# Attention scores from 49 contracted rows, two heads at a time on the two halves of the partitions

## The reference

```python
# layer 0
h = layer_norm(x) * (1 + scale) + shift          # scale, shift from the condition
scores = q @ k.T / sqrt(16) - torus_dist * torus_scale[head]
x = x + softmax(where(mask, scores, -1e30)) @ v @ Wout
x = x + gelu(layer_norm(x) @ W1 + b1) @ W2 + b2
# layer 1
scores = where(node_mask, q @ k.T / sqrt(16), -inf)
x = x + gate * modulate(layernorm(softmax(scores) @ v @ proj_w + proj_b))
x = x + gate * modulate(layernorm(gelu(x @ fc1_w + fc1_b) @ fc2_w + fc2_b))
```

## Time and profile before

| | |
|---|---|
| median of 3 runs | 1530.71 us (1530.26 to 1530.89) |
| profiled execution | 1530.74 us, of it 1528.9 between first and last instruction |
| mean granted TensorE clock | 0.96 of full |
| PE / PEld busy | 1372.1 / 1090.1 us |
| DVE / ACT / POOL busy | 866.8 / 803.0 / 692.0 us |
| first score product of turn 0 | at 43.42 us |
| scores of layer 0 | until 869.7 us, of layer 1 from 887.6 us |

### The profile page before, as it was taken

How to read it: one execution, slowest core, us unless ns; L and a number is a source line. 1 busy time by engine, 2 the same in 40 slices (tenths; PEclk the granted TensorE clock), 3 DMA queues, 4 the chain that set the end, 5 groups by cost and what they waited for, 6 DMA issues and landing times.

```text
span 1528.9 us, 25914 instructions
## 1 busy us (share of the span) xinstructions
PE 1372.1 (90%) x9365; PEld 1090.1 (71%) x9365; DVE 866.8 (57%) x2296; ACT 803.0 (53%) x1266; POOL 692.0 (45%) x856
## 2 busy tenths in 40 slices
PE   5898999999999999999999978898979888888867
PEld 3666777777777777777777767676767677767655
DVE  3766647548548457466556454647384746465551
ACT  3556655756746746656657526362535444453611
POOL 2788767758658758668768510101010101010110
PEclk9999999999999999999999989998999998999988
DMA  8654426325425534345263275856665747474510
GB/s 252 109 112 76 92 29 98 84 30 98 98 41 79 103 55 72 84 76 98 37 117 85 29 161 84 180 89 137 93 154 73 160 62 166 56 158 79 69 42 14
DMA packets 102537, 142.56 MB, mean 93 GB/s; under 512 B 22114, under 2 KB 49906, under 8 KB 102402
## 3 DMA queue, kind: packets, MB, share of 16 engines
q1 hardware_dynamic: 102402, 140.82, 49.6%
HBM read 98.27 MB, written 41.98 MB: 92 GB/s over the span
## 4 chain that ended last, share of the span: by engine, by line
PE 56%; DVE 18%; ACT 12%; POOL 7%; issue 3%; DMA 2%; SPq 1%; DVEq 0%; ACTq 0%; POOLq 0%
PE dense L589 15%; PE dense L569 13%; PE turned L669 9%; DVE shifted L1082 5%; PE pv L684 5%; PE score L657 4%; POOL shifted L472 3%; PE score L703 3%; ACT hidden L853 2%; PE turned L712 2%; POOL bias L465 2%; ACT L853 2%; DVE stats L968 2%; ACT L888 2%; DVE x_norm L978 2%
## 5 line engine op out<-in xcount | busy, mean ns | idle before, releaser
L1082 DVE CUSTOM_DVE_ANT_0 shifted<-score,bias 128x512 f32<-128x512 f32 x512 | 332.7, 687 | 258.4 <-PE score L657 156.8
L472 POOL TENSOR_SCALAR shifted<-shifted,row_max 128x512 f32<-128x512 f32 x512 | 358.3, 712 | 222.1 <-DVE row_max L1082 219.9
L872 ACT ACTIVATE probs<-turned 128x512 f32<-128x512 f32 x512 | 278.1, 596 | 213.3 <-PE turned L669 211.7
L669 PE MATMUL turned<-ident,shifted 128*128 128x128 f32 x2048 | 269.7, 274 | 7.5 <-POOL shifted L472 6.8
L669 PEld LDWEIGHTS turned<-ident,shifted 128*128 128x128 f32 x2048 | 233.3, 141 | 56.5 <-issue 26.7
L589 PE MATMUL dense<-w_down,hidden 128*128 128x256 f32 x1024 | 247.0, 385 | 12.1 <-ACT hidden L853 12.1
L465 POOL TENSOR_SCALAR bias<-dist,scale 128x1024 f32<-128x1024 f32 x192 | 218.4, 1138 | 21.0 <-DMA down_bias<-in_L_cond_b 21.0
L657 PE MATMUL score<-k_rows,q_rows 65*128 65x512 f32 x512 | 205.3, 456 | 23.6 <-DVE row_max L1082 10.5
L589 PEld LDWEIGHTS dense<-w_down,hidden 128*128 128x128 f32 x1024 | 185.6, 191 | 51.1 <-issue 16.3
L569 PE MATMUL dense<-feat_m,w_up 128*128 128x512 f32 x768 | 192.7, 404 | 8.4 <-DVE feat_m L1046 6.1
L888 ACT ACTIVATE probs<-turned 128x512 f32<-128x512 f32 x128 | 76.4, 597 | 202.8 <-PE turned L712 202.4
(11 more groups left out here) (114 smaller groups left out, 1556.6 us busy)
## 6 DMA issues: line engine op xcount, KB each, us to landing
q_rows<-qk_halves SPq DMA_DIRECT2D x256, 128.0 KB
k_rows<-qk_halves SPq DMA_DIRECT2D x256, 128.0 KB
qk_halves<-qk_high SPq DMA_DIRECT2D x64, 256.0 KB, 3.0
qk_halves<-qk_low SPq DMA_DIRECT2D x64, 256.0 KB, 3.0
x_in_t<-in_x SPq DMA_DIRECT2D x8, 512.0 KB, 3.6
x_res<-in_x SPq DMA_DIRECT2D x8, 512.0 KB, 8.3
x_mid<-x_norm SPq DMA_DIRECT2D x8, 512.0 KB, 3.5
x_in_t<-x_mid SPq DMA_DIRECT2D x8, 512.0 KB, 9.1
```

The costliest lines, as they stand in the source:

```text
L472: ins = pool.tensor_scalar(shifted[:, u % 3, i, :], shifted[:, u % 3, i, :], -1.0, row_max[:, t % 6:t % 6 + 1], ALU.mult, ALU.add)
L669: mm = pe.transpose(turned_bank[z % 2][:, HALF * kk + P * i:HALF * kk + P * i + P], shifted[:, u % 3, i, P * kt:P * kt + P], ident[:, :])
L872: act.activation(probs[:, u % RING, 2 * pair:2 * pair + 2, :], turned_bank[z % 2][:, :].rearrange("p (a c) -> p a c", a=2), ACT.Exp)\
L1082: dve.tensor_tensor_reduce(shifted[:, u % 3, i, :], score_bank[t % 2], bias[:, u % 2, i, :], 1.0, 3.0e38, ALU.add, ALU.min, row_max[:, t % ...
```

## The change

- The low x low term goes: 3 x 16 rows and the mask's row, 49 in place of 65.
- Even heads lie on partitions 0 to 48 and odd heads on 64 to 112 of `q_rows` and `k_rows`. A group is loaded by 14 transfers instead of 9 (12 of 16 rows by two heads, two of the mask's row). The ones are set on two ranges of 32 partitions.
- A unit of layer 0 is now one tile of 128 queries of two heads (`unit(u)`), in the two banks as before. Both its products wait until both tiles of the unit before have been read.
- Its bias is made by two instructions of 128 x 512, since the scale differs by head.
- `pv` takes its 256 queries from two units (two runs of 128 columns).
- In layer 1 the scores of two heads are made at even steps, one head to a bank, 4 pairs of products of 256, 256, 256 and 128 columns.

```diff
-    KROWS = 4 * HD
+    TERMS = ((0, 0), (0, 1), (1, 0))
+    KROWS = len(TERMS) * HD
+    STRIP = P // 2
-    ROWS_LOADED = 9 * 16
+    ROWS_LOADED = 2 * (2 * len(TERMS) + 1) * 16
+    def unit(u):
+        return HG * (u // 8) + 2 * (u % 4 // 2), 2 * (u // 4 % 2) + u % 2
...
-        q_rows = sb("q_rows", [KROWS + 1, 2, HG, L], F32R)
-        k_rows = sb("k_rows", [KROWS + 1, 2, HG, L], F32R)
+        q_rows = sb("q_rows", [P, 2, HG // 2, L], F32R)
+        k_rows = sb("k_rows", [P, 2, HG // 2, L], F32R)
...
             def load_group(m, g):
-                for r in range(4):
-                    sp.dma_start(q_rows[HD * r:HD * r + HD, g % 2, :, :].bitcast(F32),
-                                 qk_halves[m, r // 2, 0, rows, :].rearrange("(h e) n -> e h n", e=HD))\
+                for e in range(2):
+                    for r, (x, y) in enumerate(TERMS):
+                        at = slice(STRIP * e + HD * r, STRIP * e + HD * r + HD)
+                        sp.dma_start(q_rows[at, g % 2, :, :].bitcast(F32),
+                                     qk_halves[m, x, 0, rows, :].rearrange("(h a e) n -> a e h n", a=2, e=HD)[e])\
+                            .then_inc(loaded, 16)
...
             def make_bias(n, u):
-                pool.tensor_scalar(bias[:, u % 2, :, :], dist[:, 2 * half:2 * half + 2, :], scale[:, h:h + 1], 0.0,
-                                   ALU.mult, ALU.add).then_inc(s["bias_ready"], 1)
+                for i in range(2):
+                    ins = pool.tensor_scalar(bias[:, u % 2, i, :], dist[:, tile, :], scale[:, h + i:h + i + 1], 0.0,
+                                             ALU.mult, ALU.add)
+                ins.then_inc(s["bias_ready"], 1)
...
             def scores(n, u):
+                if n > 0 or u > 0:
+                    pe.wait_ge(s["scores_used"], TILES * n + 2 * u)
                 for i in range(2):
-                    t = 2 * u + i
-                    if n > 0 or t > 1:
-                        pe.wait_ge(s["scores_used"], TILES * n + t - 1)
-                    q0 = HALF * half + P * i
-                    pe.matmul(score_bank[t % 2], q_rows[:, g % 2, j, q0:q0 + P],
-                              k_rows[:, g % 2, j, :], start=True, stop=True).then_inc(s["scores_ready"], 1)
+                    at = slice(STRIP * i, STRIP * i + KROWS + 1)
+                    pe.matmul(score_bank[i], q_rows[at, g % 2, pair, P * tile:P * tile + P],
+                              k_rows[at, g % 2, pair, :], start=True, stop=True).then_inc(s["scores_ready"], 1)
...
             def attend(n, gq):
+                        slot = (4 * gq + j // 2 * 2) % RING
-                                       probs[:, (4 * gq + j) % RING, kt, :], start=(kt == 0), stop=(kt == TT - 1),
+                                       probs[:, slot:slot + 2, kt, P * (j % 2):P * (j % 2) + P], start=(kt == 0), stop=(kt == TT - 1),
...
             def head_scores_of(n, h):
                 pe.wait_ge(s["scores_used"], TILES * n + TT * h)
-                for t in range(TT):
-                    mm = pe.matmul(score[:, t // 2, HALF * (t % 2):HALF * (t % 2) + HALF],
-                                   q_rows[:, g % 2, j, P * t:P * t + P], k_rows[:, g % 2, j, L - HALF:L],
-                                   start=True, stop=True)
-                mm.then_inc(s["scores_ready"], TT)
+                for t in reversed(range(TT)):
+                    first = max(t - 1, 0)
+                    for i in range(2):
+                        at = slice(STRIP * i, STRIP * i + KROWS + 1)
+                        mm = pe.matmul(score_bank[i][:, P * first:P * t + P],
+                                       q_rows[at, g % 2, pair, P * t:P * t + P],
+                                       k_rows[at, g % 2, pair, L - P * (t + 1 - first):L], start=True, stop=True)
+                mm.then_inc(s["scores_ready"], 2 * TT)
...
-                        if k < H:
+                        if k < H and k % 2 == 0:
                             head_scores_of(n, k)
```

More of the change, by code:

```diff
@@ L127, in build @@
         score_bank = [score[:, i, :] for i in range(2)]
-        head_scores = score[:, :, :].rearrange("p a b -> p (a b)").rearrange("p (t k) -> p t k", t=TT)[:, :, HALF - P:HALF]
+        head_scores = [score[:, i, :].rearrange("p (t k) -> p t k", t=TT) for i in range(2)]
         turned_bank = [ps(f"turned{i}") for i in range(2)]
@@ L294, in load_mask @@
                 rows = d["mask_BxS_bf1"] if m < B else d["mask_BxS_bk0"]
-                sp.dma_start(mask_row[KROWS:KROWS + 1, :], rows[m % B:m % B + 1, :]).then_inc(s["mask_loaded"], 16)
+                sp.dma_start(mask_row[:, :], rows[m % B:m % B + 1, :]).then_inc(s["mask_loaded"], 16)
                 if m >= B:
@@ L317, in load_group @@
                 rows = slice(HG * HD * g, HG * HD * (g + 1))
-                for r in range(4):
-                    sp.dma_start(q_rows[HD * r:HD * r + HD, g % 2, :, :].bitcast(F32),
-                                 qk_halves[m, r // 2, 0, rows, :].rearrange("(h e) n -> e h n", e=HD))\
-                        .then_inc(loaded, 16)
[L322 to L327, removed]
+                for e in range(2):
[4 more added lines that the diff above has]
+                            .then_inc(loaded, 16)
+                        sp.dma_start(k_rows[at, g % 2, :, :].bitcast(F32),
+                                     qk_halves[m, y, 1, rows, :].rearrange("(h a e) n -> a e h n", a=2, e=HD)[e])\
+                            .then_inc(loaded, 16)
+                    at = STRIP * e + KROWS
+                    sp.dma_start(k_rows[at:at + 1, g % 2, :, :].bitcast(F32),
+                                 mask_neg[:, :].bitcast(F32).unsqueeze(1).broadcast_to([1, HG // 2, L]))\
+                        .then_inc(loaded, 16)
             def next_mask(m):
@@ L512, in prologue @@
                 pool.wait_ge(s["pool_consts"], 3)
-                pool.memset(q_rows[KROWS:KROWS + 1, :, :, :].bitcast(F32), 1.0).then_inc(s["ones_set"], 1)
-                pool.wait_ge(s["ones_set"], 1)
+                for e in range(2):
+                    pool.memset(q_rows[STRIP * e + 32:STRIP * e + STRIP, :, :, :].bitcast(F32), 1.0)\
+                        .then_inc(s["ones_set"], 1)
+                pool.wait_ge(s["ones_set"], 2)
                 mask(0)
@@ L648, in scores @@
             def scores(n, u):
[L649 removed]
+                h, tile = unit(u)
+                g, pair = h // HG, h % HG // 2
                 if u % 8 == 0:
                     rows_loaded(n, g)
+                if n > 0 or u > 0:
+                    pe.wait_ge(s["scores_used"], TILES * n + 2 * u)
                 for i in range(2):
[L653 to L658 removed]
+                    at = slice(STRIP * i, STRIP * i + KROWS + 1)
+                    pe.matmul(score_bank[i], q_rows[at, g % 2, pair, P * tile:P * tile + P],
+                              k_rows[at, g % 2, pair, :], start=True, stop=True).then_inc(s["scores_ready"], 1)
             def turn_unit(n, u):
@@ L856, in make_bias @@
             def make_bias(n, u):
-                h = HG * (u // 8) + u % 4
-                half = u // 4 % 2
+                h, tile = unit(u)
                 if n > 0 or u > 1:
                     act.wait_ge(s["scores_used"], TILES * n + 2 * u - 2)
-                act.activation(bias[:, u % 2, :, :], dist[:, 2 * half:2 * half + 2, :], ACT.Copy,
-                               scale=scale[:, h:h + 1]).then_inc(s["act_bias_ready"], 1)
+                for i in range(2):
+                    ins = act.activation(bias[:, u % 2, i, :], dist[:, tile, :], ACT.Copy, scale=scale[:, h + i:h + i + 1])
+                ins.then_inc(s["act_bias_ready"], 1)
             def exps(n, u):
```

21 lines of the change are left out of this document (10 added, 11 removed).

## The result

The changed kernel takes 1543.8 us, median of 4 runs (1541.6 to 1547.0); the kernel before took 1530.5 on the same chip (4 runs, 1529.9 to 1530.9). The ratio is 1.0089, with an interval of 1.0067 to 1.0111: slower by 13 us. The profiled execution took 1547.0 us with a span of 1545.1, so it is the longest of the four, and its differences from before are some 3 us larger than those of the medians.

The account below looks back on a forecast made before the run. It took the first layer as bound by TensorE's instruction stream, the second by a chain that changes engines. Against 1530.74 us, +28 (first layer) - 16 (second) + 1 (loading) = +13: 1544 us; whole range 1506 to 1566.

Parts of the forecast that it names:

- Step 1: Layer 0's split score pair on TensorE: edges make it 0.12 us longer per pair, 0.035 less where `pv` follows.
- The 0.38 among the signs: Sign in the profile after: transposes come 0.38 us from where the score pair starts to stream.
- Free edges: Rival: the row split needs no emptying of the array, weights are still loaded ahead; 1502 us, chance 0.17.
- half price: Rival: the array is drained at the split's edges, but weights are preloaded; 1525 us, chance 0.18.
- Strips in turn: Rival: strips load one after the other, each pair has 0.10 more exposed; 1561 us, chance 0.13.
- no sharing: Rival: a pair's two products share nothing, 0.235 us more for some 19 pairs; 1584 us, chance 0.06.
- Step 2: Layer 0's wait for both tiles: 0.62 us added VectorE idle per place; 1.0, 0.8 and 0.8 late at three stretches.
- less rounding: Deduction for places that overlap, in layer 0's sum 1.0 + 0.8 + 0.8 + 0.9 + 0.15, giving +3.5 us a turn.
- Step 3: Two-instruction bias in layer 0: GpSimd's +0.29 us each mostly ready in time; two ScalarE biases on the chain, +0.15 a turn.
- GpSimd becomes what VectorE waits for: Sign that would show the forecast wrong: VectorE waiting for GpSimd, whose bias was put near 0.7 us twice.
- Step 4: Layer 1's scores of both heads at even steps, none at odd: -2.0 us a turn, 8 turns, -16 us.
- Step 5: Loading before the first score product: +2.3 us if issue decides, -2.6 if bytes do; taken as +1.

Follow-up runs that it names:

- the first experiment: The changed kernel, but in layer 0 each score product waits for its own bank alone: 1528.2 us, ratio 1.0012 to the kernel before.
- bias alone: The kernel before, with each bias made by two instructions of 128x512 on GpSimd and ScalarE and nothing else: 1539.6 us, ratio 1.0076.
- 49 rows alone: The kernel before, low x low term left out, 49 rows contracted from partition 0 for every head, products one after another: 1589.8 us, ratio 1.0406.
- no split: The changed kernel, but layer 0's score products contract rows 0 to 112, so the array is not split there: 1539.3 us, ratio 1.0068 to the kernel before.
- both-tile wait alone: The kernel before, with both score products of a unit waiting until both tiles of the unit before are read: 1556.3 us, ratio 1.018.
- three terms over 65 rows: The kernel before, low x low term left out, still 65 rows with rows 48 to 63 zeros, 7 transfers for 9: 1523.9 us, ratio 0.9971.

## Why the prediction was right, and where its terms were not

**The time.** 1544.0 predicted, 1543.8 measured; a layer-0 turn of 111.1 predicted, 111.3 measured. The forecast's mechanism holds in kind: edges on both sides of each pair cost more than the sharing gives, the wait for both tiles costs more than they do, and layer 1 gives back some 40%. The total is nearer than its terms deserve. In the profiled execution layer 0 lost 31.6 us for 28, layer 1 gained 12.8 for 16, and the start gained 2.55 where 1 was to be lost.

**Step 1, the pair on TensorE: right, 0.12 predicted, 0.13 measured.** By parts: entry 0.10, not 0.20; from the pair's start to the transposes 0.43, where the sum had 0.235 and 0.10; behind it 0.05, as put. (The 0.38 among the signs takes in that 0.05, which doesn't lie there.) Where `pv` follows it is 0.42 after an entry of 0.10, for 0.47 and 0.10: 0.05 less, put at 0.035. For a turn I had 1.06, 0.86 after the waits for ScalarE; the first experiment less the bias alone gives 109.9 - 108.68 = 1.2. That is a difference, not a run: no run has the split pairs alone, and edges and bias overlap in part (the table below, unit 13). Taken out of the whole change they are worth only 0.16. *Free edges* (1502) and *half price* (1525) are out by the run of 49 rows alone, which pays 0.35 a pair with nothing shared. *Strips in turn* (1561) and *no sharing* (1584) are out by the pair's 0.50 us, as long as one product, and by 0.43 against 0.66. By the Trainium skill's page "TensorEngine Tiling (Array Packing)", section Key Properties, a change of the tiling mode drains TensorE; the run with 49 rows agrees, and shows that a lone product in rows 0 to 48 is enough for it.

**Step 2, the wait: its stretches right, its size alone too low.** The idle time per place was put at 0.62 (its terms, 0.54 and 0.10, make 0.64) and is 0.69. How late the transposes of a unit are in turn 4, against the same unit of before, counted from the turn's start (us):

| unit | 0 | 7 | 12 | 13 | 18 | 19 | 21 | 23 | 31 |
|---|---|---|---|---|---|---|---|---|---|
| changed kernel | 0.51 | 0.92 | 1.35 | 1.35 | 1.62 | 2.19 | 2.42 | 3.10 | 3.53 |
| each bank's own wait | -0.09 | 0.37 | 0.80 | 1.02 | 1.30 | 1.38 | 1.61 | 1.74 | 2.16 |
| no split | 0.84 | 1.13 | 1.13 | 1.57 | 1.98 | 2.55 | 2.75 | 3.53 | 3.51 |
| both-tile wait alone | 0.84 | 1.72 | 1.72 | 1.73 | 1.97 | 2.54 | 2.75 | 3.35 | 3.33 |
| bias alone | 0.00 | 0.23 | 0.24 | 0.68 | 0.86 | 0.86 | 0.87 | 1.05 | 1.05 |

The edges are what rises by some 0.1 a unit from 8 to 12 and from 24 on: of these five only the two kernels with split pairs have it (0.43 and 0.43 in the changed one, where I had put 0.9 in all). The wait is what the first row has over the second: 0.60 at unit 0, 0.49 more at 19 and 0.55 more at 22 and 23. The bias is the step at 13, and the changed kernel doesn't have it. The second group of four norm instructions, near unit 13, takes 1.44 us before, 2.15 with GpSimd's bias alone split and 1.87 without the row split, but 1.58 in the changed kernel: there it starts so late that GpSimd's work ends 0.48 us after it began. Without the split the turn loses 0.44 there, and 0.21 each up to unit 7 and from 13 to 23 against the changed kernel. That makes up for the 0.86 of the edges, so that it ends as late.

I had put 1.0 by unit 7, 0.8 at 20 and 21 and 0.8 at 24 and 25. The changed kernel is 0.92 late at unit 7, loses 0.80 from 19 to 21 and 0.68 at 22 and 23, so the stretches are one or two units off. But alone the wait costs 3.33, and on top of the other parts only 1.4 (111.32 - 109.9). The edges by that difference, the wait and the bias sum to 1.2 + 3.33 + 1.05 = 5.6 a turn, the change to 3.7. What a turn has lost to one cause the next can't take again in full. My sum had no such overlap except "less rounding", and terms too small by about as much: it put all three at 3.65. So the size came out right by two errors that cancel. That is luck, and not that each term was known. VectorE's wait for scores shows it: +15 us predicted, +54 measured (156.8 to 210.7). That is 6.7 a turn, more than the turn grew, so most of it does not set the turn. Its wait for GpSimd's bias fell at the same time, from 21.5 to 2.0 us.

**Step 3, the bias: mis-sized.** 0.15 a turn predicted, 1.05 measured. I had costed ScalarE's two biases on the chain and held GpSimd's for covered. ScalarE's is worth 0.41 alone and GpSimd's 0.95. GpSimd's duration was right (690 ns twice, put at 0.7); ScalarE's went up by 0.18 us a bias (73.6 to 85.2 us busy for 64), put at 0.08. What I left out is that a longer busy GpSimd slows VectorE's norm instructions, which lie on the chain near units 5 and 13 (the table's step of 0.44). The 0.24 that stands there by unit 7 I put down to GpSimd's bias of unit 2 coming late, which no run takes apart; VectorE's wait for GpSimd's bias did grow, by 19.4 us. In the changed kernel that wait is 2.0 us, so the sign "GpSimd becomes what VectorE waits for" didn't show there, though the cost did in the parts.

**Step 4, layer 1: right.** -2.0 a turn predicted. 69.7 for 71.6 at equal granted clock is -1.9, and -12.2 over seven turns (495.0 for 507.1, both of one chip) is -1.7. Of the profiled execution's -12.8 the last stretch takes back 0.9. The wait of the earlier trace rows in layer 1 went as put. The groups by shape of the changed kernel, columns as in the earlier trace rows:

```profile
L1134 DVE TENSOR_REDUCE row_max<-score 128x4 f32<-128x512 f32 x128 | 87.1, 681 | 90.6 <-PE score L722 90.6
...
L722 PE MATMUL score<-k_rows,q_rows 49*128 49x256 f32 x384 | 42.7, 330 | 13.2 <-DVE shifted L1136 9.5 <-issue 3.6
...
L722 PEld LDWEIGHTS score<-k_rows,q_rows 49*128 49x128 f32 x512 | 37.5, 200 | 33.8 <-issue 24.3 <-DVE shifted L1136 9.3
```

TensorE's waits for VectorE before the scores are 9.5 and 9.3 us, for 52.4 and 62.9. So half of the steps no longer make the round from VectorE to TensorE and back. One even step in order of time:

```profile
1140.10 0.69 DVE L1136 TENSOR_TENSOR shifted<-score,row_max 128x512 f32<-128x512 f32 x1
...
1140.85 0.69 PE L722 MATMUL score<-k_rows,q_rows 49*128 49x256 f32 x8 [1.44 <-DVE shifted L1136]
...
1141.46 0.66 PE L731 MATMUL turned<-ident,shifted 128*128 128x128 f32 x4
```

Here TensorE had been waiting 1.44 us when VectorE was done, and the turning of the head before comes 0.61 after the eight products start: that is the even step's price, paid once for two heads.

**Step 5, loading: mis-sized, +1 predicted, -2.55 measured.** I took a middle between bytes and issues; bytes decide. The kernel with 7 transfers of 128 KB and the changed one with 14 of 64 KB have their first score product at the same time, 40.81 and 40.87. SyncE and TensorE in order of time, in the changed kernel:

```profile
38.67 0.59 SPq L336 DMA_DIRECT2D k_rows<-mask_neg  x1
...
40.87 0.79 PE L671 MATMUL score<-k_rows,q_rows 49*128 49x512 f32 x2 [3.24 <-DMA k_rows<-mask_neg]
```

The last issue comes 2.4 us later than in the earlier trace rows, and its landing 2.2 us after it instead of 7.0.

## What to carry to other kernels

Before contracting fewer rows, look at what stands around the product: here 49-row products among full ones cost 0.35 us more per pair of products, and running two at once gave back only 0.23 of it. At 65 rows nothing of the kind shows; where between 49 and 65 it sets in was not measured. When two results share one wait, count the round trip between the engines (0.69 us here) at each place where the consumer used to go straight on, and then expect the losses of several parts to overlap: parts of 5.6 us made 3.7. Part by part, look for the one that gains by itself; here it was the order of layer 1, and put into the kernel before without the split it is worth 0.8%, with the fewer loaded bytes 1.1%.

## What the runs showed of the hardware that was not expected

**VectorE's norm instructions and GpSimd.** A norm instruction of 128 x 256 elements (SBUF to SBUF, one tensor read) lasts 0.40 us when GpSimd is idle and 0.78 beside it. Both are in the changed kernel, VectorE and GpSimd in order of time:

```profile
477.18 2.86 DVE L997 TENSOR_SCALAR x_norm<-x_in_t,mean_var,rstd 128x256 f32<-128x256 f32 x4
...
504.06 1.58 DVE L997 TENSOR_SCALAR x_norm<-x_res,mean_var,rstd 128x256 f32<-128x256 f32 x4
...
477.11 1.38 POOL L476 TENSOR_SCALAR bias<-dist,scale 128x512 f32<-128x512 f32 x2
478.49 1.40 POOL L484 TENSOR_SCALAR shifted<-shifted,row_max 128x512 f32<-128x512 f32 x2
...
503.15 1.38 POOL L484 TENSOR_SCALAR shifted<-shifted,row_max 128x512 f32<-128x512 f32 x2
```

Beside GpSimd's work without a gap, one norm instruction starts every 0.70 us, GpSimd's own pace; once GpSimd stops at 504.5 they start every 0.32. In the busy stretch each norm instruction ends 0.15 us after one of GpSimd's (GpSimd's end at 477.80, 478.49, 479.19 and 479.89, the norm's at 477.94, 478.64, 479.34 and 480.04). The longest of all, 1130 ns in the kernel before and 1204 with the both-tile wait, lie beside a bias of 1.2 and 1.1 us. So a norm instruction seems to get through only where GpSimd goes from one instruction to the next. The Trainium skill's page "SBUF — State Buffer", section Who interferes with whom, says that VectorE's `tensor_scalar` in a mode with two ports and any GpSimd instruction take a shared pair of ports in turn, each for its whole length. The trace agrees for VectorE. GpSimd's own 1.38 to 1.40 us for two are hardly longer beside it, but a little of the reverse shows too: five biases of the kernel before that start some 0.09 us behind a norm instruction last 1221 to 1231 ns, where those with none beside them have a median of 1114.

**DMA onto both halves of the partitions.** The changed kernel and the one with three terms over 65 rows move nearly the same bytes. Their queue rows (packets, MB, share of 16 engines), the changed kernel first:

```profile
q1 hardware_dynamic: 98306, 124.06, 27.2%
```

```profile
q1 hardware_dynamic: 92162, 124.03, 39.6%
```

The same 124 MB take 27% of the engines' time when the rows go to partitions 0 to 48 and 64 to 112, and 40% when all go to 0 to 47 and 64. It bought no time: the first score product, which waits for such loads, comes at 40.87 and 40.81. By the Trainium skill's page "SBUF — State Buffer", section Door 1: The DMA port swizzle, partitions 64 above each other go through different ports; the two rows agree with it, but no run here varied the partitions alone, since the transfers are also of 64 KB in one and of 128 KB in the other.
